# Attention maxima reduced and transposed by half groups, eight units later; PSUM copies and the last loads placed elsewhere

## What is computed

```python
def _L0_attn_ref(x, W_qkv, W_o):
    b, L, _ = x.shape
    qkv = jnp.einsum('bld,ed->ble', x, W_qkv)
    qkv = qkv.reshape(b, 3, H, L, D_H)              # H = 16 heads of D_H = 32
    Q, K, V = (qkv[:, 0], qkv[:, 1], qkv[:, 2])
    scores = jnp.einsum('bhqd,bhkd->bhqk', Q, K) * D_H ** (-0.5)
    attn = jax.nn.softmax(scores, axis=-1)
    out = jnp.einsum('bhqk,bhkd->bhqd', attn, V)
    out = out.transpose(0, 2, 1, 3).reshape(b, L, D_IN)
    return jnp.einsum('bld,ed->ble', out, W_o)
```

## Time and profile before

| | us |
|---|---|
| median of three runs | 3299.98 |
| time of the profiled execution | 3298.3 |
| its span, first to last instruction | 3296.5 |
| weight and token stages | up to about 1510 |
| maxima alone, ahead of the first score | 1520.4 to 1566.2 |
| 32 groups, to the first full-width product of the output stage | 1566.2 to 3132.9 |
| output projection of the other 15 tiles | 3132.9 to 3296.5 |

### The profile page before, as it was taken

How to read it: one execution, slowest core, us unless ns; L and a number is a source line. 1 busy time by engine, 2 the same in 40 slices (tenths; PEclk the granted TensorE clock), 3 DMA queues, 4 the chain that set the end, 5 groups by cost and what they waited for, 6 DMA issues and landing times.

```text
span 3296.5 us, 73574 instructions
## 1 busy us (share of the span) xinstructions
PE 3230.9 (98%) x30468; PEld 1552.7 (47%) x30468; DVE 2433.6 (74%) x3472; ACT 1992.1 (60%) x2969; POOL 1828.3 (55%) x659
## 2 busy tenths in 40 slices
PE   5999999999999999998999999999999999999899
PEld 4444444444444444442444444444444444544344
DVE  6777666666666777667888888888888888888544
ACT  6444443444444444440888888888888888888711
POOL 0333322323233333320888988988988998898800
PEclk8999999999999999996999999999999999999999
DMA  4132222222222223224443443344343343332296
GB/s 179 77 84 102 77 90 82 85 92 75 97 70 100 61 103 83 103 56 86 76 77 74 87 79 78 77 86 78 71 90 76 73 85 80 75 82 61 75 340 233
DMA packets 376191, 309.36 MB, mean 94 GB/s; under 512 B 300800, under 2 KB 317184, under 8 KB 365568
## 3 DMA queue, kind: packets, MB, share of 16 engines
q1 hardware_dynamic: 375872, 304.69, 34.5%
HBM read 96.99 MB, written 139.46 MB: 72 GB/s over the span
## 4 chain that ended last, share of the span: by engine, by line
PE 49%; issue 1%; DVE 1%; POOL 1%; DMA 1%; ACT 1%; SPq 0%; POOLq 0%; ACTq 0%; DVEq 0%
PE es_for_maxima_and_scores L1204 27%; PE outputs L1225 13%; PE misc L1259 6%; PE es_for_maxima_and_scores L1300 3%; DVE half_maxima L1135 1%; POOL probs_sum L1051 1%; ACT probs L1083 0%; DMA k_stackT<-attention_scratch 0%; PE misc L1242 0%; DMA q_stackT<-stack_scratch 0%; POOL out_normed L1058 0%; DVE q_stackT L1158 0%; ACT k_stackT L1094 0%; ACT k_stackT L1089 0%; DMA q_stackT<-maxima_rows 0%
## 5 line engine op out<-in xcount | busy, mean ns | idle before, releaser
L1135 DVE TENSOR_REDUCE half_maxima<-es_for_maxima_and_scores 128x1 f32<-128x512 f32 x2048 | 1275.8, 683 | 249.0 <-PE es_for_maxima_and_scores L1204 233.3
L1083 ACT ACTIVATE probs<-es_for_maxima_and_scores,scalars 128x512 f32<-128x512 f32 x2048 | 1248.2, 696 | 316.2 <-PE es_for_maxima_and_scores L1204 312.7
L1051 POOL TENSOR_TENSOR probs_sum<-probs_sum,probs 128x2048 f32<-128x2048 f32 x224 | 1026.3, 4582 | 23.8 <-POOL probs_sum L1051 0.4
L1204 PE MATMUL es_for_maxima_and_scores<-k_stackT,q_stackT 96*32 96x512 f16 x8192 | 852.9, 389 | 11.9 <-DMA q_stackT<-stack_scratch 11.1
L1204 PE MATMUL es_for_maxima_and_scores<-q_stackT,k_stackT 98*32 98x512 f16 x8192 | 841.7, 384 | 9.3 <-issue 6.9
L1225 PE MATMUL outputs<-probs,v_rows 128*32 128x512 f32 x4096 | 539.2, 594 | 2.2 <-ACT probs L1083 0.8
L525 POOL TENSOR_TENSOR gelu_sum<-gelu_sum,gelu_out 128x1024 f32<-128x1024 f32 x96 | 254.6, 2652 | 451.8 <-ACT gelu_out L696 451.8
L1204 PEld LDWEIGHTS es_for_maxima_and_scores<-q_stackT,k_stackT 98*32 98x32 f16 x8192 | 327.4, 137 | 348.7 <-ACT probs L1083 108.2
L1051 POOL TENSOR_TENSOR probs_sum<-probs 128x2048 f32<-128x2048 f32 x64 | 293.2, 4581 | 225.8 <-ACT probs L1083 225.8
L1204 PEld LDWEIGHTS es_for_maxima_and_scores<-k_stackT,q_stackT 96*32 96x32 f16 x8192 | 245.7, 96 | 313.1 <-DVE half_maxima L1135 174.8
L758 PE MATMUL psA<-tile_xh,ternary_fcT 128*128 128x512 f16 x1024 | 388.1, 379 | 1.1 <-PEq L87 1.1
(11 more groups left out here) (162 smaller groups left out, 3344.5 us busy)
## 6 DMA issues: line engine op xcount, KB each, us to landing
stack_scratch<-hi_hi_lo_hi_rows SPq DMA_DIRECT2D x32, 1536.0 KB, 5.1
stack_scratch<-hi_hi_lo_hi_rows SPq DMA_DIRECT2D x32, 576.0 KB, 6.0
v_scratch<-v_rows_out SPq DMA_DIRECT2D x32, 576.0 KB, 6.9
tile_xs<-in_L_attn_x SPq DMA_DIRECT2D x16, 1024.0 KB, 4.8
x_plus_ffn_scratch<-tile_xs SPq DMA_DIRECT2D x16, 1024.0 KB, 3.9
v_rows<-v_scratch SPq DMA_DIRECT2D x32, 512.0 KB, 4.4
inverse_denominators<-denominators_scratch SPq DMA_DIRECT2D x256, 64.0 KB, 2.0
attention_scratch<-out_normed SPq DMA_DIRECT2D x64, 256.0 KB, 2.0
```

What stands on the lines that cost most here:

```text
L1051: nc.gpsimd.tensor_tensor(acc[:, hf], pr[:, 0] if j == 1 else acc[:, hf], pr[:, j], ALU.add).then_inc(added, 1)
L1083: nc.scalar.activation(pr[:, w % 8, h, :], psS[:, bank(g, HG * w + h), :], ACT.Exp, scale=keep["scal"]["escale"]).then_inc(exp_done, 1)
L1135: nc.vector.tensor_reduce(mx[:, slot(n, 2), h, t, kh:kh + 1], psX[:, bank(n, r), :], axis=AX.X, op=ALU.max).then_inc(max_done, 1)
L1204: last = nc.tensor.matmul(out[q:q + 32, :], stationary[:, q:q + 32], moving, start=start, stop=stop)
```

## The change

The maxima of a group are taken in another order: first all that concern the first half of the queries (32 of them, `place`), then the second half. With `X_LATE = 5` they are made in units 5 to 15 of the group ahead and 0 to 4 of the group itself. The body of group -2 is gone. After 32 maxima the half is negated, split and moved, in unit 13 for the next group's first half and in unit 5 for the own second half. The split into two fp16 numbers is now done by DVE ahead of the transposition, on 16 columns. The transposition is 4 matmuls in fp16, one for each column group of 32 (one head each), against an fp16 unit matrix. ACT, not DVE, copies the result (128 x 128) out of PSUM, between the third and the fourth exponential of the unit. The rows of a head now lie in partitions 32h + 4a + t, so SP moves them with 8 DMAs per half, each with 4 source rows of 256 bytes, 16 a group in place of 2. `scores(g, 0, 0)` waits for the first half's 8 and `scores(g, 8, 0)` for the second half's 8.

`collect` and ACT's copy of denominators go from units 5 and 13 to 4 and 12, there from after the first exponential to after the third. The last group's maxima take its units 0 to 4, so its share of the output projection starts in unit 5 instead of 2 and 4 products follow after the loop. The casts and subtractions for it start in units 2 and 3 instead of 0 and 1. The first loads of the output stage go from unit 10 to unit 15 of group 30, both attention tiles first.

```diff
-X_LATE = 13
+X_LATE = 5
 PER_GROUP = 2 * KT_N * HG
+PER_HALF = PER_GROUP // 2
-COLLECT = {5: (1, 1), 13: (0, 0)}
+COLLECT = {4: (1, 1), 12: (0, 0)}
...
-DEN_OUT = {5: (1, 1), 13: (0, 0)}
+DEN_OUT = {4: (1, 1), 12: (0, 0)}
...
-ROWS_AT = 14
+ROWS_AT = {5: (0, 1), 13: (1, 0)}
 TILES = B * L // TT
-HIGH_AT = 0
-LOW_AT = 1
-PROJECT_AT = 2
+HIGH_AT = 2
+LOW_AT = 3
+PROJECT_AT = 5
...
-            body(-2, range(X_LATE, UNITS))
             body(-1, range(UNITS))
...
+        def place(r):
+
+            hf, k = divmod(r, PER_HALF)
+            h, t, kh = k // KT_N, k % KT_N // 2, k % 2
+            return h, hf * (KT_N // 2) + t, kh
...
-            ahead, first = (1, w + UNITS - X_LATE) if w < X_LATE else (2, w - X_LATE)
+            ahead, first = (0, w + UNITS - X_LATE) if w < X_LATE else (1, w - X_LATE)
...
-            def load_maxima(n):
-                sp.wait_ge(rows_ready, lin(n, 1, 1))
+            def load_maxima(n, hf):
+                sp.wait_ge(rows_ready, lin(n, 2, hf + 1))
                 for a in range(2):
-                    sp.dma_start(qT[STACK + a:STACK + a + 1, slot(n, 4)].rearrange("a h (t c) -> a (h t) c", c=P),
-                                 rows[:, a, :]).then_inc(aug_loaded, 16)
+                    for t in range(KT_N // 2):
+                        first = hf * BANK + t * P
+                        sp.dma_start(qT[STACK + a:STACK + a + 1, slot(n, 4), :, first:first + P],
+                                     rows[4 * a + t:P:32, :]).then_inc(aug_loaded, 16)
...
-                    if g == GROUPS - 2 and w == 10:
+                    if g == GROUPS - 2 and w == 15:
                         sp.wait_ge(s_full, PER_GROUP * (GROUPS - 2))
                         for t in range(2):
                             load_out_tile(t)
+                        for t in range(2):
                             load_sum(t)
...
+            def maxima_rows(n, hf):
+                act.wait_ge(a_full, lin(n, 2, hf + 1))
+                wait(act, aug_loaded, lin(n, 256, 128 * hf))
+                nc.scalar.copy(rows[:], psM[:, 0:P]).then_inc(rows_ready, 1)
...
                     for h in range(HG):
+                        if h == 3 and rows_due(g, w):
+                            maxima_rows(*rows_due(g, w))
                         exp(g, w, h)
-                        if h == 0 and due(DEN_OUT, g, w):
+                        if h == 2 and due(DEN_OUT, g, w):
                             denominators(*due(DEN_OUT, g, w))
...
-            def negate(n):
-                dve.wait_ge(max_done, lin(n, PER_GROUP, PER_GROUP))
-                wait(dve, a_full, lin(n, 1))
-                nc.vector.tensor_reduce(nm[:], mx[:, slot(n, 2)].rearrange("p h t k -> p (h t) k"), axis=AX.X, op=ALU.max,
-                                        negate=True).then_inc(nm_ready, 1)
-
-            def split_rows(n):
...
+            def negate(n, hf):
+                dve.wait_ge(max_done, lin(n, PER_GROUP, PER_HALF * (hf + 1)))
+                wait(dve, nm_lo, lin(n, 2, hf))
+                part = mx[:, slot(n, 2), :, 4 * hf:4 * hf + 4, :]
+                nc.vector.tensor_reduce(nm[:], part, axis=AX.X, op=ALU.max, negate=True).then_inc(nm_ready, 1)
+                dve.wait_ge(nm_ready, lin(n, 2, hf + 1))
+                wait(dve, a_full, lin(n, 2, hf))
+                nc.vector.tensor_scalar(nm16[:, :, 0:4], nm[:], 1.0 / AUG_UNIT, None, ALU.mult).then_inc(nm_hi, 1)
+                dve.wait_ge(nm_hi, lin(n, 2, hf + 1))
+                nc.vector.scalar_tensor_tensor(nm16[:, :, 4:8], nm[:], 1.0 / AUG_UNIT, nm16[:, :, 0:4],
+                                               ALU.mult, ALU.subtract).then_inc(nm_lo, 1)
...
+                    if rows_due(g, w):
+                        negate(*rows_due(g, w))
                     for k, x in enumerate(maxima(g, w)):
...
+                if i == 0 and h == 0:
+                    pe.wait_ge(aug_loaded, lin(g, 256, 128 * hf + 128))
                 if w == 0 and h == 0:
-                    pe.wait_ge(aug_loaded, lin(g, 32, 32))
...
-                nc.tensor.transpose(psM[0:HG * KT_N, 0:P], nm[:], keep["id32"][:]).then_inc(a_full, 1)
+            def maxima_rows(n, hf):
+                pe.wait_ge(nm_lo, lin(n, 2, hf + 1))
+                wait(pe, d_out, lin(n, 2, hf - 1))
+                for h in range(HG):
+                    last = nc.tensor.matmul(psM[32 * h:32 * h + 32, 0:P], nm16[:, h, :], id16[:], start=True, stop=True)
+                last.then_inc(a_full, 1)
...
-                    if w == ROWS_AT and exists(shift(g, 1)):
-                        maxima_rows(g)
                     if exists(g) and exists(prev[0]):
                         outputs(*prev)
+                    if rows_due(g, w):
+                        maxima_rows(*rows_due(g, w))
                     if x[2]:
                         max_scores(*x[2])
...
+            for m in range(4 * (UNITS - PROJECT_AT), 12 * CD):
+                project(0, m // 12, m % 12)
```

More of the change, by code:

```diff
@@ L833, in attention_output_stage @@
         mx = sb("half_maxima", [P, 2, HG, KT_N, 2])
-        nm = sb("negated_maxima", [P, HG * KT_N])
-        rows = sb("maxima_rows", [HG * KT_N, 2, P], F16)
+        nm = sb("negated_maxima", [P, HG, KT_N // 2])
+        nm16 = sb("negated_maxima_hi_lo", [P, HG, 32], F16)
+        id16 = sb("id16_rows", [P, P], F16)
+        rows = sb("maxima_rows", [P, P], F16)
         ones = sb("unit_rows", [2, HG * L], F16)
@@ L903, in product_bank_free, with rows_due @@
             return next((k + 1 for k in range(n - 1, -1, -1) if product_bank(k) == product_bank(n)), 0)
+        def rows_due(g, w):
+            if w not in ROWS_AT:
+                return None
+            ahead, hf = ROWS_AT[w]
+            n = shift(g, ahead)
+            return (n, hf) if exists(n) else None
+        def place(r):
+            hf, k = divmod(r, PER_HALF)
+            h, t, kh = k // KT_N, k % KT_N // 2, k % 2
+            return h, hf * (KT_N // 2) + t, kh
         def halves(t, i=3):
@@ L1106, in body @@
             def body(g, units):
-                if not exists(g):
-                    return
                 for w in units:
+                    if not exists(g):
+                        if rows_due(g, w):
+                            maxima_rows(*rows_due(g, w))
+                        continue
                     for h in range(HG):
+                        if h == 3 and rows_due(g, w):
+                            maxima_rows(*rows_due(g, w))
                         exp(g, w, h)
-                        if h == 0 and due(DEN_OUT, g, w):
+                        if h == 2 and due(DEN_OUT, g, w):
                             denominators(*due(DEN_OUT, g, w))
@@ L1131, in maximum @@
                 dve.wait_ge(x_full, lin(n, PER_GROUP, r + 1))
-                h, t, kh = r // per_head, r % per_head // 2, r % 2
+                h, t, kh = place(r)
                 if r == 0:
-                    wait(dve, nm_ready, lin(n, 1, -1))
+                    wait(dve, nm_ready, lin(n, 2, -2))
                 nc.vector.tensor_reduce(mx[:, slot(n, 2), h, t, kh:kh + 1], psX[:, bank(n, r), :], axis=AX.X, op=ALU.max).then_inc(max_done, 1)
-            def negate(n):
-                dve.wait_ge(max_done, lin(n, PER_GROUP, PER_GROUP))
-                wait(dve, a_full, lin(n, 1))
-                nc.vector.tensor_reduce(nm[:], mx[:, slot(n, 2)].rearrange("p h t k -> p (h t) k"), axis=AX.X, op=ALU.max,
-                                        negate=True).then_inc(nm_ready, 1)
-            def split_rows(n):
[L1144 to L1149, removed]
+            def negate(n, hf):
[9 more added lines that the diff above has]
+                                               ALU.mult, ALU.subtract).then_inc(nm_lo, 1)
             def invert(g, hf):
@@ L1180, in body @@
                             maximum(*x)
-                        if k == 0 and w == X_LATE and exists(shift(g, 1)):
-                            negate(shift(g, 1))
                         if k == 0 and due(INVERT, g, w):
                             invert(*due(INVERT, g, w))
-                        if k == 1 and w == ROWS_AT and exists(shift(g, 1)):
-                            split_rows(shift(g, 1))
+            nc.vector.memset(nm16[:], 0.0)
+            nc.vector.tensor_copy(id16[:], keep["id32"][:]).then_inc(tiles_set, 1)
             nc.vector.memset(ones[:], AUG_UNIT).then_inc(ones_set, 1)
+            dve.wait_ge(tiles_set, 1)
             groups(dve, body)
+            add_row(0, 3)
             for t in range(1, TILES):
@@ L1229, in max_scores @@
             def max_scores(n, r):
-                h, t, kh = r // per_head, r % per_head // 2, r % 2
-                if r % per_head == 0:
+                h, t, kh = place(r)
+                if r < PER_HALF and r % KT_N == 0:
                     pe.wait_ge(qk_loaded[slot(n, 2)][h], turn(n, 32) + 32)
@@ L1247, in denominators @@
```

(8 more changed lines are left out.)

11 lines of the change are left out of this document (4 added, 7 removed).

## The result

The changed kernel takes 3676.9 us (3673.55 to 3679.77), the kernel before took 3300.2 beside it: a ratio of 1.1143, with 1.1130 to 1.1156 as its 95% interval. Forecast were 3346 us and at most 3395. The sign was right. The size and the cause were not.

What follows compares the result with a forecast made beforehand. PE's work was taken to bound a steady group of 48.6 us. The sum was 3298.3 - 15.3 (start) - 4.1 (end) + 64.5 (31 groups) + 0.9 (first group) = 3344.3, 3346 on the median's scale; range 3274 to 3395.

Steps and rivals of the forecast that it cites:

- the price of DVE's chain: Steady group, units 5 and 13: three small DVE instructions, about 0.27 us each, costing PE 0 to 0.3 us each time.
- The start: Before the first score: fewer maxima, then 8 row DMAs; first score at 1550.9, a gain of 15.3 us.
- SP's queue: Steady group: 8 row DMAs issue late, making PE wait 1.6 us at unit 8, 0.5 at unit 0; chance 0.45.
- 14q - 6.04: Growth of a steady group in us, q being the pitch between row DMA issues; 2.08 at q = 0.58.
- PE's and DVE's work: Steady group: fp32 transposition (0.28 us) and 0.46 in unit 14 go; two fp16 transpositions come at 0.1 each.
- the quick rival: Short row DMAs issue quickly, pitch 0.37: group 0.25 us shorter to 0.3 longer, about 3279 us; chance 0.28.
- the third rival: SP quick enough, DVE's small instructions in units 5 and 13 cost PE 0.3 us each time; 3285 to 3316; chance 0.12.
- The end: Last group: the 6.35 us gap and 2.2 of slow clock go, extra max scores cost 4.4; gain 4.1 us.
- Its counter-argument: Against the case that DVE holds PE: the present split stops DVE in unit 14 as long, no later unit shows it.
- A wait of PE so long that the granted clock falls: Warning sign: long PE waits could lower its clock and make the time worse than forecast; no size given.

Runs made afterwards that it cites:

- stt: The changed kernel with the fp16 high part made by scalar_tensor_tensor, with two SBUF inputs, in place of tensor_scalar: 3676.42 us, ratio 1.1141.
- psum: The changed kernel with the negated maxima kept in the transpositions' PSUM bank instead of SBUF: 3318.67 us, ratio 1.0062.
- psum_wide: As psum, with a head's 512 maxima transposed into one partition, so 2 row DMAs per half instead of 8: 3282.99 us, ratio 0.9951.
- psum_store5: As psum, with the output's store of unit 3 moved to unit 5, behind the rows in SP's queue: 3290.25 us, ratio 0.9972.
- before_late: The kernel before with only the last loads moved to unit 14 of group 30, projection one unit later: 3293.32 us, ratio 0.9982.
- poolhalf: The changed kernel with each of POOL's additions made in two instructions of half the length: 3665.97 us in a single run.
- before_tiny: The kernel before with one unread DVE scaling of 128 x 16, SBUF to SBUF, added in a group: 3454.04 us, ratio 1.0465.

## Why the prediction was wrong, point by point

**The step that failed** is the price of DVE's chain: "One such costs about 0.27", with 0 to 0.3 us for PE. In its place stand 4.1 us of DVE and 6.6 of PE, each time. The row was of a `tensor_scalar`, as was the new instruction, but with its source in PSUM ("maxima_rows<-misc"), while the new one reads and writes SBUF. The trace of before had the right row, in the token stage. There the same operation between two SBUF tiles stands now alone and now beside a POOL addition:

```profile
169.06 0.76 DVE L593 TENSOR_SCALAR h_hi<-gelu_out,scalars 128x1024 f16<-128x1024 f32 x1 [3.14 <-ACT gelu_out L696]
...
175.03 2.95 DVE L593 TENSOR_SCALAR h_hi<-gelu_out,scalars 128x1024 f16<-128x1024 f32 x1 [2.12 <-ACT gelu_out L696]
...
175.07 2.35 POOL L525 TENSOR_TENSOR gelu_sum<-gelu_out 128x1024 f32<-128x1024 f32 x1 [31.05 <-ACT gelu_out L696]
```

0.76 alone, 2.95 beside POOL's 2.35. The view of that line gives 752/754/2956 ns as minimum, median and maximum; 45 of its 128 take over 2.2 us. A maximum near the minimum plus a POOL instruction, with a POOL addition of 4.6 us in a group, was the number to carry over.

The Trainium skill says it in "SBUF — State Buffer", section "Who interferes with whom": DVE and GpSimd share one port pair, and it is an exclusive lock, held for the whole instruction. Operations such as `tensor_scalar` can enter the mode that takes both ports; one with two SBUF inputs contends too; `tensor_reduce` never does. These runs agree: the reduction L1170 takes 0.19 at all times, L1173 4.1, the two-input form of stt 4.1, and psum's pair with a PSUM operand 0.17. The one instruction of after that seems to go against it, L1175 with two SBUF inputs, is taken up below. I didn't weigh that page in the forecast.

**The start.** Forecast: first score at 1550.9, a gain of 15.3. It stands at 1548.92, a gain of 17.2. The constant rows came at 1542.89 instead of 1544.20 (this differs from run to run: 1545.08 in psum_wide), the pitch was 0.54, and the last DMA was seen 1.6 us after its issue, not 1.95.

**SP's queue.** Right as a mechanism, too large in size, and hidden in the changed kernel. The issues take 492 ns (median), a pitch of 0.537 where 0.58 was taken. With it the forecast's 14q - 6.04 gives 1.48 us a group. The group of psum is 49.56 us long (2013.92 to 2063.48), that of psum_store5 48.66 (2008.47 to 2057.13): 0.9. So without DVE's waits the forecast's own sum, with the measured q, gives some 3327, and psum took 3318.7. The last DMA is seen 1.6 us after its issue (2015.51 + 7 x 0.537 to 2020.91), not 1.95. For unit 0 the 0.2 that this q gives is at most 0.1. In after itself the rows cost PE nothing in a steady group: they are issued behind the gap (2022.43), and PE at half clock takes longer to the next first score than they do to land.

**PE's and DVE's work.** Where neither POOL nor a late DMA holds anything up, the groups are 48.66 (psum_store5) and 48.80 us (psum_wide) long, not the 48.35 of the quick rival (0.25 less than 48.6), which has nothing for DVE. In psum's unit 5 two pairs of scores stand 0.10 and 0.15 us further apart (2014.64 to 2014.96, 2015.19 to 2015.56, against 0.22). So an unblocked chain costs PE about 0.25 each time, near the 0.3 of the third rival. ACT's copy took 0.27 us (0.3 assumed). The four matmuls of a transposition hold the next score up by 0.06 (2013.92 to 2013.98; 0.1 assumed).

**The end.** Forecast: 4.1 us gained. before_late shows 6.0 (0.9 to 2.8 per mille) without the extra maxima, for which the forecast's terms give 8.5. The gap of 2.64 us at 3085.29, which before doesn't have, is about the difference. In psum_wide start, groups and end together give -15.5 us of span: -18.1 for the start, +6.2 for 31 groups that are 0.2 longer, which leaves -3.6 for the end. Its last group has three gaps of about 1 us behind DVE that weren't foreseen.

**The rivals.** The third named DVE as the engine that holds PE, which is what happened, at 0.3 us instead of 6.6. Its counter-argument, that the present split stops DVE as long and nothing shows, rested on the same row with its PSUM source. No case allowed for a small instruction to be as long as POOL's. "A wait of PE so long that the granted clock falls would make it worse than said" came true: 3.0 of each 6.6.

**The second small instruction.** L1175 of after has two SBUF inputs and never waits (0.17), while in poolhalf its counterpart does (2.26). The start times settle it. In after POOL's next addition starts 0.07 to 0.08 us behind L1175 (2021.55 and 2021.63 above), in 62 of 64 cases, and in the other 2 not within 2 us. In poolhalf POOL's next half stands directly behind the last one and has been running for 0.10 to 0.13 us (2015.81 for POOL, 2015.91 for DVE above) in all 56 cases that wait. In the 8 that take 0.17 it starts 0.08 behind, and once none is near. So what counts for this pair is whether POOL's instruction is already running. That isn't the whole rule: the rows of L593 that wait for 2.95 us start 0.04 ahead of POOL's. How two starts that close are decided stays open.

## What to carry to other kernels

A small DVE instruction is to be priced by where its operands lie and by what POOL is doing, not by its size alone. Before a small one is put on SBUF tiles beside a long POOL instruction, look in the trace for the maximum of the same form there. If PE waits for it, move its source to PSUM (of two inputs, one was enough here), or the instruction out of POOL's way, and count the slower clock behind the gap with the wait.

## What the runs showed that I had not expected

- A scaling of 16 elements per partition took up to 4.45 us, 25 times its 0.175, because an addition of 4.6 us was running on another engine. That was in before_tiny. In psum the same operation with its source in PSUM took 0.175 beside the same additions.
- Cutting POOL's instruction in half didn't shorten the stall, since the second small instruction then waited as well (2.27 + 2.26 for 4.12).
- In the row at 175.03 DVE started 0.04 us ahead of POOL and was still the one that waited.
- Gaps of 3.6 us brought PE's granted clock to 0.50 for about 6 us each time. The gap of 0.6 in psum left the windows at 1.00.
